# ScalarE's order in a recurrence over batches: two copies ahead of the next normalising

## The chip, the core and the metric

The kernel runs on one core of a Trainium2 chip. The metric is the device time of one execution in microseconds; the lower the better. The core has five instruction queues that run by themselves and meet only at semaphores: TensorE (PE, with its weight loads as PEld), VectorE (DVE), ScalarE (ACT), GpSimd (POOL) and SyncE (SP). Each queue is worked off strictly in the order in which it was written.

## The reference, cut to what matters

The input x has 8 batches of 512 rows of 128 values. Three layers follow one another: a mixture of experts, a linear recurrence along the rows, and the mixture of experts again with the same weights.

```python
x = x + 0.5 * ffn(layernorm(x), gate_w, w1, w2)
x = x + attn(layernorm(x), a_params, B_w, C_w, D)
x = x + 0.5 * ffn(layernorm(x), gate_w, w1, w2)

def attn(u, ...):            # per batch; W is a circulant matrix, so it is diagonal after an FFT
    Bu = einsum('bsd,nd->bsn', u, B_w)
    h_t = ifft(lambdas * fft(h_{t-1})).real + Bu_t
    return einsum('sbn,dn->bsd', hs, C_w) + D * u

def ffn(tokens, ...):        # 8 experts, each token to its best one, at most 160 tokens an expert
    logits = tokens @ gate_w; probs = softmax(logits); expert = argmax(probs)
    pos = running count of the tokens of that expert
    out = probs[expert] * relu(token @ w1[expert]) @ w2[expert]   # if pos < 160
```

## The kernel before

The first expert layer fills the first 62 us, the recurrence the stretch from 62 to about 120, and the second expert layer the rest. The change touches the recurrence alone.

The recurrence is worked in the frequency domain, where every state is one complex number that is turned by a fixed angle at each step. A batch is cut into 128 groups (NG) of 4 rows (TB). The state at the group boundaries comes from a scan over group sums that have been turned back to a common origin, and the rows within a group come from small tables. For each batch b of the 8 (NB) this happens, in this order of data:

- VectorE, `stats(b)`: mean and variance of the rows (sstat, smv). ScalarE, `deviation(b)`: the square root (ssd, L433). VectorE, `shift(b)`: reciprocal and shift (srs, snb, L715 and L716).
- ScalarE, `normalise(b)`: u, four instructions of 128x128 (L440). TensorE, `turn_u(b)`: four transposes into bank 4 (L977). ScalarE, `copy_uT(b)`: uT, one copy of 128x512 (L427).
- TensorE, `group_sums(b)`: the sums of the groups into bank 5 (L986, four matmuls that the trace counts as eight).
- ScalarE, `turned_part(b)`: two copies of 64x128 that swap the real and imaginary halves of bank 5 into vq (L419, L420). They need the group sums (semaphore v_ps) and GpSimd's product of the batch before (vb_r).
- VectorE, `turn_back(b)`: va = bank 5 times cosines (L722), once vq is there. GpSimd: vb = vq times sines (L339).
- VectorE, `carry(b)`: the scan z over va and vb (L730), then zs (L734). GpSimd: zc (L344). VectorE, `turn_forth(b)`: state = zc + zs (L743).
- TensorE, `read_out(b)`: state times a table into the batch's pair of banks (L1020), on top of `within_pairs(b)` (L997 to L1001) and `within_rest(b)` (L1008 to L1012), the products within the groups.
- VectorE, `add_back(b)` (L748) and `gate_back(b)` (L758, L761): the result with the residual, and the logits of the second expert layer. SP stores each batch.

The order of each queue is written out by hand. VectorE's loop for batch i is `turn_back(i)`, `stats(i + 2)`, `carry(i)`, `turn_forth(i)`, `add_back(i - 1)`, `gate_back(i - 1)`, `shift(i + 2)`, and in batches 3 to 6 a share of the routing of the second expert layer (`mark`, L540 to L587, and `make_hot`, L604 to L623). TensorE's loop is `group_sums(i)`, `read_out(i - 1)`, `within_pairs(i)`, `turn_u(i + 1)`, `within_rest(i)`; after batch 5 it ranks the first routed piece (`rank`, L864 to L871), after batch 7 it places it (`place`, L879), then ranks the second and reads out the last batch. `within_pairs(i)` waits until VectorE has read the batch two before it out of the same banks. GpSimd's loop is vb of the batch, then zc of the batch. `keep_warm` (L804) issues matmuls whose result is not used.

After the recurrence the last routing steps follow one another on VectorE and TensorE, then an indirect load by GpSimd (L317), then the experts (L910, L921).

Of the kernel before, what the change touches and what calls it, by code (L numbers as in the profile page):

```python
# [5 lines left out]
def macaron_moe_ssm_kernel(nc, x_in, x_turned, a_params, b_w, c_w, c_w_turned, d_skip, gate_w, w1, w2,  # L6
# [11 lines left out]

    NB, SEQ, D = x_in.shape
    E, _, F = w1.shape  # L20
    P = 128
    T = NB * SEQ
# [24 lines left out]
    with ctx:  # L47
# [301 lines left out]
        def _(act):  # L349
# [33 lines left out]
            def slots(n):  # L383
                def slot_in(j):
                    act.wait_ge(slotT_ps, n * NS + j + 1)
                    nc.scalar.copy(xcT[:, j * P:(j + 1) * P],  # L386
                                   bank[j % 2][:, 0:P]).then_inc(slotT_sb, 1)

                def relu(e):
                    for half in range(2):  # L390
                        act.wait_ge(h_ps, n * 2 * E + 2 * e + half + 1)
                        if e >= 2:
                            act.wait_ge(eo_ps, n * E + e - 1)
                        nc.scalar.activation(hT[:, e % 2, half * HC:(half + 1) * HC, :],  # L394
                                             bank[4 + half][:, 0:HC * CAP]
                                             .rearrange("p (c s) -> p c s", c=HC), ACT.Relu).then_inc(h_sb, 1)

                for kind, i in act_steps:
                    if kind == "i":
                        slot_in(i)  # L400
                    elif kind == "g":
                        act.wait_ge(rated, n * NS + NS)
                        nc.scalar.activation(gsd[:, :], gmv[:, :, 1], ACT.Sqrt, bias=eps[:, 0:1]).then_inc(gsd_r, 1)
                        nc.scalar.activation(table_load[:, 1:2], eps[:, 0:1], ACT.Exp)
                    elif kind == "e":
                        act.wait_ge(lg_r, n + 1)
                        nc.scalar.activation(pe_[:, :, :], lg[:, :, :], ACT.Exp).then_inc(pe_r, 1)
                    else:
                        relu(i)
# [3 lines left out]
            def turned_part(b):  # L413

                act.wait_ge(v_ps, b + 1)
                if b >= 1:
                    act.wait_ge(vb_r, b)
                v = bank[5][:, 0:NG]
                nc.scalar.copy(vq[0:P // 2, :], v[P // 2:P, :])  # L419
                nc.scalar.copy(vq[P // 2:P, :], v[0:P // 2, :]).then_inc(vq_sb, 1)  # L420

            def copy_uT(b):

                act.wait_ge(uT_ps, b + 1)
                if b >= 2:
                    act.wait_ge(lag_ps, b - 1)
                nc.scalar.copy(uT[:, b % 2, :], bank[4][:, :]).then_inc(uT_sb, 1)  # L427

            def deviation(b):
                act.wait_ge(svar, b + 1)  # L430
                if b >= 4:
                    act.wait_ge(y_read, b - 3)
                nc.scalar.activation(ssd[:, b % 4, :], smv[:, b % 2, :, 1], ACT.Sqrt, bias=eps[:, 0:1]).then_inc(ssd_r, 1)  # L433

            def normalise(b):
                act.wait_ge(snb_r, b + 1)
                if b >= 2:
                    act.wait_ge(uT_ps, b - 1)
                for c in range(TB):
                    ins = nc.scalar.activation(u[:, b % 2, c, :], x1[:, b * TB + c, :], ACT.Identity,  # L440
                                               bias=snb[:, b % 2, c:c + 1], scale=srs[:, b % 2, c:c + 1])
                ins.then_inc(u_r, 1)
# [3 lines left out]
            normalise(0)  # L446
            copy_uT(0)
            normalise(1)
            for i in range(NB):
                turned_part(i)  # L450
                if i + 1 < NB:
                    copy_uT(i + 1)
                if i + 2 < NB:
                    deviation(i + 2)
                    normalise(i + 2)
            slots(1)

# [648 lines left out]
```

## Time and profile before

| | us |
|---|---|
| median of 3 runs | 175.39 |
| lowest and highest | 174.82, 181.41 |
| the profiled execution | 176.61 |
| its span, first to last instruction | 174.7 |

The profile is of one execution. Times within it are microseconds from the first instruction. TensorE's clock has two levels, 1.2 and 2.4 GHz; a granted clock of 1.00 is the upper one and 0.50 the lower. Busy shares over the span are 80% for TensorE, 51% for VectorE, 33% for ScalarE and 30% for GpSimd.

### The profile page before, as it was taken

The page shows a single profiled execution, that of the slowest core. Times are in us where ns is not written, and L with a number is a line of the kernel's source. Part 1 is how long each engine was busy: PE and PEld are TensorE (multiplying, and loading weights), DVE is VectorE, ACT ScalarE, POOL GpSimd, SP SyncE. Part 2 cuts the span into 40 slices and gives each one's busy share as a digit, 9 for nine tenths or more (in the row PEclk, how much of TensorE's full clock was granted, in tenths as well). Part 3 has the DMA queues.
Part 4 walks back from the last instruction along what each step waited for, and adds up shares of the span by engine and source line. Part 5 has one row for each costly group of instructions (what it writes and reads, how often), then busy time and mean ns, then how long its engine had stood idle before and what let it go on. Part 6 is the DMA issues. An engine that isn't in the chain of part 4 may idle for free.

```text
span 174.7 us, 2535 instructions
## 1 busy us (share of the span) xinstructions
PE 140.6 (80%) x788; PEld 104.8 (60%) x791; DVE 89.7 (51%) x396; ACT 58.2 (33%) x144; POOL 52.9 (30%) x80
## 2 busy tenths in 40 slices
PE   6977899989999787499788888896439969999920
PEld 2137468389998432388566666675234448999810
DVE  1069762984474206065485597698464134434320
ACT  3421143634736000846525525510000013483200
POOL 3700001776047720022012012121000477305771
PEclk9998589999999999999999999999555987999995
DMA  4999990111001129300101100111010011100110
GB/s 133 314 364 362 372 560 19 45 45 51 9 19 58 51 51 323 141 2 0 60 25 39 60 38 23 62 60 64 0 60 0 13 47 45 45 4 31 46 45 30
DMA packets 11309, 16.21 MB, mean 93 GB/s; under 512 B 1665, under 2 KB 6273, under 8 KB 11265
## 3 DMA queue, kind: packets, MB, share of 16 engines
q1 hardware_dynamic: 9504, 13.11, 21.4%
q0 software_dynamic: 1280, 2.62, 5.0%
q10 hardware_dynamic: 512, 0.33, 0.7%
q8 instruction: 6, 0.10, 0.2%
q14 instruction: 7, 0.05, 0.1%
HBM read 12.65 MB, written 5.51 MB: 104 GB/s over the span
## 4 chain that ended last, share of the span: by engine, by line
PE 41%; DVE 24%; issue 10%; ACT 8%; DMA 8%; POOL 5%; SPq 1%; POOLq 1%; DVEq 0%; ACTq 0%
PE pair L910 11%; PE pair L921 9%; ACT u L440 5%; PE pair L852 5%; DVE sstat L701 4%; PE pair L879 4%; DMA xt<-x_turned 3%; PE pair L804 3%; DVE x L748 2%; PE pair L899 2%; POOL zc L344 2%; DVE smv L706 2%; DVE z L730 2%; DMA x<-x_scratch 2%; DMA xg<-out,tok 2%
## 5 line engine op out<-in xcount | busy, mean ns | idle before, releaser
L804 PE MATMUL pair<-warm_in,ones_bf 128*128 128x512 bf16 x77 | 21.7, 428 | 4.2 <-DVE warm_in L469 1.6
L910 PE MATMUL pair<-xcT,w1s 128*128 128x160 f32 x128 | 21.8, 316 | 0.0
L921 PE MATMUL pair<-hT,w2s 128*128 128x160 f32 x128 | 20.5, 303 | 0.8 <-ACT hT L394 0.8
L910 PEld LDWEIGHTS pair<-xcT,w1s 128*128 128x128 f32 x128 | 18.9, 199 | 0.8 <-ACT xcT L386 0.8
L394 ACT ACTIVATE hT<-pair 128x320 f32<-128x320 f32 x32 | 13.7, 436 | 16.4 <-PE pair L910 15.0
L921 PEld LDWEIGHTS pair<-hT,w2s 128*128 128x128 f32 x128 | 18.1, 192 | 1.5 <-ACT hT L394 0.8
L440 ACT ACTIVATE u<-x,snb,srs 128x128 f32<-128x128 f32 x32 | 13.2, 482 | 13.4 <-DVE snb L716 13.4
L317 POOL DMA_INDIRECT xg<-x,tok x10 | 10.2, 1024 | 23.7 <-DVE tok L638 20.9
L317 POOL DMA_INDIRECT xg<-out,tok x10 | 10.1, 1006 | 22.0 <-DVE tok L638 19.2
L804 PEld LDWEIGHTS pair<-warm_in,ones_bf 128*128 128x128 bf16 x80 | 8.3, 110 | 13.7 <-issue 3.3
L386 ACT COPY xcT<-pair 128x128 f32<-128x128 f32 x20 | 4.9, 266 | 31.3 <-PE pair L894 31.2
L339 POOL TENSOR_TENSOR vb<-vq,st 128x128 f32<-128x128 f32 x8 | 3.6, 455 | 37.3 <-ACT vq L420 37.3
L1020 PE MATMUL pair<-gt,state 128*128 128x272 f32 x32 | 10.4, 453 | 3.8 <-DVE state L743 3.8
L326 POOL DMA_INDIRECT out<-xnew,tok x10 | 9.9, 988 | 10.7 <-DVE xnew L682 8.9
L326 POOL DMA_INDIRECT x_scratch<-xnew,tok x10 | 9.9, 986 | 9.8 <-DVE xnew L682 7.9
L645 DVE BATCH_NORM_STATS2 gstat<-xg 128x6 f32<-128x128 f32 x20 | 5.7, 287 | 12.4 <-DMA xg<-out,tok 9.2
L879 PEld LDWEIGHTS pair<-hot_tok,hot_place 128*64 128x64 f16 x64 | 7.4, 202 | 7.8 <-DVE hot_place L623 6.1
L879 PE MATMUL pair<-hot_tok,hot_place 128*64 128x20 f16 x64 | 7.8, 265 | 5.3 <-DVE hot_place L623 5.3
L701 DVE BATCH_NORM_STATS2 sstat<-x 128x6 f32<-128x128 f32 x32 | 6.9, 278 | 6.9 <-DMA x<-x_scratch 6.9
L722 DVE TENSOR_TENSOR va<-pair,ct 128x128 f32<-128x128 f32 x8 | 2.3, 291 | 15.1 <-ACT vq L420 15.1
L672 DVE COPY eoT<-pair 128x160 f32<-128x160 f32 x16 | 5.1, 318 | 9.3 <-PE pair L921 9.3
L852 PE MATMUL pair<-w1s,center 128*128 128x512 f32 x16 | 9.6, 754 | 0.0
(170 smaller groups left out, 247.1 us busy)
## 6 DMA issues: line engine op xcount, KB each, us to landing
xt<-x_turned SPq DMA_DIRECT2D x8, 256.0 KB, 6.0
w1s<-w SPq DMA_DIRECT2D x2, 1024.0 KB, 7.5
w2s<-w SPq DMA_DIRECT2D x8, 256.0 KB, 6.7
x<-x_scratch SPq DMA_DIRECT2D x8, 256.0 KB, 4.5
out<-x SPq DMA_DIRECT2D x8, 256.0 KB, 2.0
ce<-const_early ACTq DMA_DIRECT2D x1, 318.0 KB, 4.4
cl<-const_late SPq DMA_DIRECT2D x1, 256.0 KB, 5.5
xg<-x,tok POOLq DMA_INDIRECT x10, 2.6
```

The lines of the kernel that those rows point to most:

```text
L317: pool.indirect_dma_start(xg[:, j, :], None, (x_rows, out_rows)[n], bass.IndirectOffsetOnAxis(ap=tok[:, j:j + 1], axis=0), bounds_check=T ...
L326: pool.indirect_dma_start((x1_dram, out_rows)[n], bass.IndirectOffsetOnAxis(ap=tok[:, j:j + 1], axis=0), xnew[:, j, :], None, bounds_check ...
L394: nc.scalar.activation(hT[:, e % 2, half * HC:(half + 1) * HC, :], bank[4 + half][:, 0:HC * CAP] .rearrange("p (c s) -> p c s", c=HC), ACT ...
L440: ins = nc.scalar.activation(u[:, b % 2, c, :], x1[:, b * TB + c, :], ACT.Identity, bias=snb[:, b % 2, c:c + 1], scale=srs[:, b % 2, c:c + 1])
L645: link(V.bn_stats(gstat[:, j, :], xg[:, j, :]))
L701: ins = V.bn_stats(sstat[:, b % 2, c, :], x1[:, b * TB + c, :])
L804: M(bank[to][:, :], ones_bf[:, :], warm_in[:, :], start=True, stop=True)
L852: M(bank[e % 2][:, :], center[:, :], w1s[:, e, :], start=True, stop=True).then_inc(w1c_ps, 1)
L879: ins = M(bank[7][0:SW, 0:NSTRIP], hot_place[:, :, t], hot_tok[:, :, t], start=(t == 0), stop=(t == NT - 1))
L910: ins = M(bank[4 + half][:, c * CAP:(c + 1) * CAP], w1s[:, i, ch * P:(ch + 1) * P], xcT[:, i * CAP:(i + 1) * CAP], start=True, stop=True)
L921: ins = M(bank[6 + i % 2][:, 0:CAP], w2s[:, i, c, :], hT[:, i % 2, c, :], start=(c == 0), stop=(c == FC - 1))
L1020: ins = M(y[:, h, E:E + 2 * PITCH], state[:, b % 2, :], gt[:, 2 * h:2 * h + 2, :].rearrange("p r c -> p (r c)"), start=False, stop=True, s ...
```

## The change

In ScalarE's loop over the batches, the two copies of batch i + 1 (`turned_part`) are issued ahead of `normalise(i + 2)`, where before they were issued after it, as the first step of the next round. The same instructions are issued, as often as before, on the same data and with the same semaphores. ScalarE's order before is copies 0, uT 1, deviation 2, normalise 2, copies 1, uT 2, deviation 3, normalise 3, copies 2 and so on; after the change it is copies 0, uT 1, deviation 2, copies 1, normalise 2, uT 2, deviation 3, copies 2, normalise 3 and so on.

```diff
             normalise(0)
             copy_uT(0)
             normalise(1)
+            turned_part(0)
             for i in range(NB):
-                turned_part(i)
                 if i + 1 < NB:
                     copy_uT(i + 1)
                 if i + 2 < NB:
                     deviation(i + 2)
+                if i + 1 < NB:
+                    turned_part(i + 1)
+                if i + 2 < NB:
                     normalise(i + 2)
             slots(1)
```

## Rows read from the trace of the kernel before

**Rows 1.** The page: TensorE's granted clock in 40 slices of 4.4 us, in tenths.

```profile
PEclk9998589999999999999999999999555987999995
```

**Rows 2.** Table of waits, 82 to 126 us: total, times, longest.

```profile
POOL vb L339 <- ACT vq L420: 21.5, 6, 4.1
ACT u L440 <- DVE snb L716: 12.0, 5, 2.4
```

**Rows 3.** Chain of waits, 92 to 107 us: shares by line, then start, us, what.

```profile
by line: ACT u L440 25.3%; DVE sstat L701 14.8%; issue 11.9%; DVE x L748 8.0%; POOL zc L344 7.6%; ACT vq L420 5.3%; ACT vq L419 5.2%; DVE smv L706 4.7%; DVE z L730 4.3%; DVE state L743 3.9%; DVE srs L715 2.5%; DVE lgu L758 2.3%; DVE snb L71
```

**Rows 4.** Timeline, ScalarE: start, us, engine, line, instruction, count [idle before, releaser].

```profile
78.38 1.65 ACT L440 ACTIVATE u<-x,snb,srs 128x128 f32<-128x128 f32 x4 [1.41 <-DVE snb L716]
...
99.69 0.26 ACT L420 COPY vq<-pair 64x128 f32<-64x128 f32 x1
...
104.26 1.65 ACT L440 ACTIVATE u<-x,snb,srs 128x128 f32<-128x128 f32 x4 [2.40 <-DVE snb L716]
105.93 0.26 ACT L419 COPY vq<-pair 64x128 f32<-64x128 f32 x1
106.20 0.26 ACT L420 COPY vq<-pair 64x128 f32<-64x128 f32 x1
```

**Rows 5.** Timeline, TensorE, from the group sums of batch 1 to those of 2.

```profile
76.86 1.05 PE L986 MATMUL pair<-uT,vt 128*128 128x128 f32 x8
...
78.11 1.18 PE L1020 MATMUL pair<-gt,state 128*128 128x272 f32 x4 [0.20 <-DVE state L743]
...
80.31 0.60 PE L977 MATMUL pair<-ce,u 128*128 128x128 f32 x4
...
81.92 1.05 PE L986 MATMUL pair<-uT,vt 128*128 128x128 f32 x8
```

**Rows 6.** Timeline, VectorE (and GpSimd's vb), batches 4 to 7.

```profile
100.05 0.29 DVE L722 TENSOR_TENSOR va<-pair,ct 128x128 f32<-128x128 f32 x1 [1.89 <-ACT vq L420]
...
104.06 0.16 DVE L716 SCALAR_TENSOR_TENSOR snb<-smv,srs 128x4 f32<-128x4 f32 x1
...
105.28 0.36 DVE L587 TENSOR_TENSOR_SCAN counted<-restart,chosen 128x96 bf16<-128x96 bf16 x1
...
106.50 0.29 DVE L722 TENSOR_TENSOR va<-pair,ct 128x128 f32<-128x128 f32 x1 [0.86 <-ACT vq L420]
...
111.80 0.17 DVE L614 TENSOR_SCALAR split_i<-slot_i 128x12 int16<-128x12 int16 x1
...
113.00 0.46 POOL L339 TENSOR_TENSOR vb<-vq,st 128x128 f32<-128x128 f32 x1 [4.07 <-ACT vq L420]
113.02 0.29 DVE L722 TENSOR_TENSOR va<-pair,ct 128x128 f32<-128x128 f32 x1 [1.05 <-ACT vq L420]
...
113.54 0.43 DVE L730 TENSOR_TENSOR_SCAN z<-va,vb 128x128 f32<-128x128 f32 x1 [0.23 <-POOL vb L339]
...
117.40 0.43 DVE L730 TENSOR_TENSOR_SCAN z<-va,vb 128x128 f32<-128x128 f32 x1
```

**Rows 7.** Timeline, TensorE, the ranking of piece 1 and the last read-out.

```profile
121.96 0.22 PE L864 MATMUL pair<-counted,ones_bf 128*128 128x96 bf16 x1 [1.73 <-DVE counted L587]
...
122.19 2.15 PE L1020 MATMUL pair<-gt,state 128*128 128x272 f32 x4
```

**Rows 8.** Stretches: length, busy (x count) of PE, PEld, DVE, ACT, POOL; PEclk, DMA, GB/s.

```profile
122.00:123.00 1.00, 1.00 (x6) 0.88 (x7) 0.00 (x0) 0.00 (x0) 0.00 (x0) 0.53 0.00 0
...
143.00:146.00 3.00, 2.69 (x11) 2.23 (x10) 1.29 (x6) 1.03 (x3) 2.38 (x3) 0.51 0.16 44
```

**Rows 9.** Timeline, the tail: the last placing and its operand; expert matmuls.

```profile
133.28 0.42 DVE L623 TENSOR_TENSOR hot_place<-split_i,place_no 128x512 f16<-128x512 int16 x1
...
134.85 1.06 PE L879 MATMUL pair<-hot_tok,hot_place 128*64 128x20 f16 x8
...
142.45 2.45 PE L910 MATMUL pair<-xcT,w1s 128*128 128x160 f32 x8
...
146.96 1.25 PE L910 MATMUL pair<-xcT,w1s 128*128 128x160 f32 x8
```

## The prediction

> **What bounds the kernel now.** I read four views, from the coarse to the fine. The page says that no engine is full over the span and that TensorE's clock is at its upper level all through the recurrence, slices 15 to 27 [rows 1]. Utilisation therefore decides nothing there; the order of waits does. The table of waits for the recurrence is next: GpSimd stands before its first product for ScalarE's copies, 21.5 us in six batches, while ScalarE stands for VectorE's snb before normalising, 12.0 us in five [rows 2]. Each waits for the other in turn: that is a ring. The chain of waits for two batches shows it closed: normalising is its largest link, a quarter of the stretch, and the two copies follow it directly [rows 3]. In the timeline, normalising of batch 6 runs from 104.26 to 105.91, the copies of batch 5 from 105.93 to 106.46, with nothing between them; the copies of batch 4 ended at 99.95, so one batch takes 6.51 us [rows 4]. Yet the group sums that those copies turn leave TensorE much earlier. In batch 1, they ended at 77.91 (76.86 + 1.05) [rows 5], before normalising of batch 2 was done. So the copies wait for nothing that they read: they wait for their place in ScalarE's queue.
>
> The ring now, from rows: VectorE from va to snb 4.17 (100.05 to 104.22) [rows 6], hand-over 0.04, four normalisings 1.65, hand-over 0.02, two copies 0.53, hand-over 0.10 (99.95 to 100.05). Sum 6.51, as measured. The account is complete. For hand-overs that the change makes new I take 0.05 between engines and 0.02 within one.
>
> **The change, part by part.** It moves two copies (0.53 us together) ahead of four normalisings (1.65 us). It adds and removes no instruction, no DMA and no semaphore; nothing moves on SP, GpSimd, VectorE or TensorE. Four edits follow from the one.
>
> (a) The copies leave the ring of VectorE and normalising. For batch 1 they now start when the group sums are there: 77.91 + 0.05 = 77.96, done 78.49, and va of batch 1 starts at 78.55.
>
> (b) A new wait stands ahead of normalising: ScalarE stands for the group sums of the batch before. Queued behind that wait are the four normalisings, the transposes on TensorE that read u, and the next copy of uT. For batch 2 this costs little: normalising would start at 78.38 as before [rows 4], the copies hold it to 78.51, so u ends at 80.16; TensorE is not free for those transposes before 80.31 anyway [rows 5]. The 0.13 is hidden by TensorE's own queue. So the group sums of batch 2 end as before, at 82.97, its copies at 83.55, and va starts at 83.60.
>
> (c) From there a new ring decides: transposes to the end of the group sums 2.66 (80.31 to 82.97) [rows 5], hand-over 0.05, copies 0.53, hand-over 0.02, normalising 1.65, hand-over 0.05. Sum 4.96. TensorE's own queue is nearly as long: group sums to group sums 5.06 with a 0.20 wait in it [rows 5], so 4.86. I take 4.96 for the ring; below 4.86 it can't go. VectorE's 4.17 is shorter for plain batches. Then va of batch 3 starts at 88.56 and of batch 4 at 93.52.
>
> (d) VectorE has routing work in later batches, and there its order becomes the bound. In batch 4, va to the end of counted is 5.59 (100.05 to 105.64) [rows 6]; with 0.03 between instructions, va of batch 5 starts at 99.14. In batch 5, va to the end of split_i is 5.47 (106.50 to 111.97): batch 6 at 104.64. Its group sums should end at 103.1 (82.97 + 4 x 4.96, and some 0.25 for the ranking matmuls ahead of them, as those of piece 1 delay the next matmul by 0.23, 121.96 to 122.19 [rows 7]), copies 103.7, hence VectorE is indeed later. Batch 6: va to z was 0.52, of which 0.23 was a wait for GpSimd's vb that goes away, so z starts at 104.93; from there to the next z VectorE works without a wait, 3.86 (113.54 to 117.40), which would be 108.79. The copies of batch 7: normalising can start at 103.7 and ends at 105.4, group sums 2.66 later at 108.1, copies 108.64. vb ends at 109.15 (0.05 and 0.46), and the scan z of batch 7 starts 0.08 later (113.46 to 113.54), at 109.2: here GpSimd is the later one. Before, it started at 117.40 [rows 6]. **The recurrence gives 8.2 us.**
>
> After that scan nothing is reordered, so the lead is carried through routing, gather and experts, with one term more, from TensorE's clock. Before, TensorE had nothing for 1.73 us ahead of the ranking of piece 1 [rows 7]; the second that follows had a mean clock of 0.53 [rows 8], and the four matmuls of the last read-out took 2.15 us, against 1.18 for the same four at the full clock [rows 5, 7]. They are on the path: VectorE waits for them. Now TensorE's queue runs later against VectorE's: after the group sums of batch 7 (108.1) come read-out and the products within the batch, 3.2 (the 4.86 of a batch less group sums 1.05 and transposes 0.60), and twelve placing matmuls, 1.6 (eight take 1.06 [rows 9]), to 112.9, while ranking follows z by the same 4.56 as before (117.40 to 121.96), at 113.8. The gap is 0.9 us in place of 1.73. I take the full rate for the read-out: 0.9 us gained. Its other bound is 0, if the clock falls at the same instruction.
>
> [...]
>
> Sum: 8.2 + 0.9 = 9.1 us. The profiled execution took 176.61 us, 1.9 more than its span; it would take 167.5. It lies 1.22 above the median of the runs, 175.39, and since the terms are differences, the forecast for the median is 175.39 - 9.1 = **166.3 us**.
>
> **The rivals.**
>
> *The tail meets a kinder clock.* Everything after the recurrence comes 8 us sooner, and the tail has two stretches at the lower level. In one, the last placing matmuls start at 134.85, although their operand was written by 133.70: they stood 1.15 behind keep-warm matmuls at half rate [rows 9]. In the other, 143 to 146 at 0.51 [rows 8], eight matmuls of expert 0 took 2.45 against 1.25 [rows 9], 1.20 more. Both spared: 163.9. For it: the smaller gap. Against it: the long wait after the last read-out remains, in which the clock had already fallen.
>
> *The tail meets a harder clock.* The read-out stays at half (0.9 back) and one more block of eight runs at half (1.2): 168.4. With two such blocks, 169.6. For it: only the order of work is fixed, not when the clock changes.
>
> *VectorE is the bound in every batch.* If its queue took 5.6 us in all batches instead of in the routed ones, va of batch 7 would come at 78.55 + 6 x 5.6 = 112.15 and z at 112.5, so the recurrence gives 4.9 and the time is 170.5 without the clock's term. Against it: 4.17 in a plain batch is a row without waits in it.
>
> *The gain is given back.* The expert stage would need 5.6 us more, five blocks at half instead of one or two: about 172.3 (166.3 + 5 x 1.2), no measurable change. A change that does nothing belongs here too (175.4): for that the group sums would have to be late, and 77.91 is against it.
>
> *Slower.* The new wait ties normalising to TensorE's pace, so a halved clock inside the recurrence would now count in full. The read-out's ratio, 2.15 / 1.18 = 1.82, makes TensorE's 4.86 into 8.85 us a batch, 3.9 over the new ring. From the fourth such batch on, the gain and the 2% are gone (9.1 + 3.5 = 12.6 against 4 x 3.9 = 15.6): 181.9. Against it: the clock is full there now, with more idle time of TensorE than afterwards.
>
> **How the numbers follow.** About 2% (3.5 us) is what a measurement of this kernel can tell from no change. Forecast, 165 to 168: 0.62. Kinder clock, 163 to 165: 0.14. Harder clock, 168 to 170: 0.13. VectorE in every batch: 0.03. Given back, or nothing done: 0.05. Slower: 0.03. All but the last two lie over 2% below 175.39, so faster 0.92, same 0.05, slower 0.03. The range runs from both clock gains (163.9, less half a microsecond for the runs' scatter) to two blocks at half (169.6, rounded up): 163.4 to 169.8. What it leaves out holds under 2 in 10.
>
> **What the profile after would show.** (a) ScalarE's two copies start some 0.05 after TensorE's group sums, with that as releaser, and no longer right after normalising. (b) Normalising starts right after the copies; the wait for snb nearly vanishes from the table and a wait for the group sums takes its place. (c) Batches 2 to 4 are about 5.0 us apart. (d) In batches 4 to 6 VectorE has no wait ahead of va, and the spacing of va is 5.6 and 5.5. The last scan starts near 109. The last read-out takes 1.2, not 2.15. The prediction is wrong if the spacing in (c) stays above 6, if group sums start late because of something in TensorE's queue that the slack of before covered, or if the granted clock in the expert stage differs for more than two blocks.

## The result, and the profile after

The changed kernel took 168.28 us (median of 4 runs, 167.04 to 169.97), against 176.44 for the kernel before beside it (median of 4, 174.82 to 181.41). The ratio is 0.9587, with a 95% interval of 0.9479 to 0.9695. In a second comparison on another occasion, the same kernel gave 0.9464 (0.9382 to 0.9545). The forecast was 166.3 us, a ratio of 0.948 to the 175.39 that it started from. Executions in which TensorE's clock is lower over the whole span are longer by some per cent for every kernel here; the ratios leave them out.

The profiled execution after took 168.07 us, with a span of 166.0, against 176.61 and 174.7 before.

First the page of the changed kernel: its span and the granted clock, to be laid beside [rows 1].

```profile
span 166.0 us, 2535 instructions
...
PEclk9998579999999999987999999999755699999995
```

A dip that was not there before stands in slices 17 and 18, at the start of the recurrence; the one in the expert stage of before (its slices 34 and 35) is missing.

The table of waits of the changed kernel, 78 to 110 us: who waited for whom, total, times, longest.

```profile
POOL vb L339 <- ACT vq L420: 15.3, 6, 2.7
ACT vq L419 <- PE pair L989: 9.4, 7, 1.5
```

The row of [rows 2] in which ScalarE waited for VectorE's snb is gone. In its place ScalarE now waits for the group sums, 1.3 us a batch. GpSimd's longest wait for the copies has gone from 4.1 to 2.7 us.

The chain of waits, 85 to 96 us (line numbers below the change are three higher): shares, then start, us, what.

```profile
by line: ACT u L440 30.1%; PE pair L989 16.5%; PE pair L980 11.9%; issue 11.3%; PE pair L1013 8.6%; PE pair L1011 8.4%; DVE sstat L704 7.9%; PE pair L1015 4.5%; ACT vq L420 2.7%; DVE va L725 1.6%; ACT vq L419 0.4%; DVEq L724 0.2%
...
85.00 1.66 ACT u L440 x4
...
86.70 0.66 PE pair L980 x4
87.36 0.46 PE pair L1011 x2
87.82 0.47 PE pair L1013 x2
88.29 0.24 PE pair L1015 x2
88.54 0.91 PE pair L989 x8
...
90.02 1.66 ACT u L440 x4
```

Beside [rows 3]: the round between two normalisings no longer passes through VectorE's scan, state and snb; it passes through the transposes, the rest of the products within the batch (L1011 to L1015) and the group sums, all on TensorE. One round goes from normalising at 85.00 to normalising at 90.02, 5.02 us.

Timeline of ScalarE, batches 1 and 2, answering to [rows 4], and of TensorE, answering to [rows 5].

```profile
78.33 1.05 PE L989 MATMUL pair<-uT,vt 128*128 128x128 f32 x8
...
83.36 1.05 PE L989 MATMUL pair<-uT,vt 128*128 128x128 f32 x8
...
84.25 1.08 PE L1023 MATMUL pair<-gt,state 128*128 128x272 f32 x4
...
84.45 0.26 ACT L419 COPY vq<-pair 64x128 f32<-64x128 f32 x1 [1.29 <-PE pair L989]
84.72 0.26 ACT L420 COPY vq<-pair 64x128 f32<-64x128 f32 x1
85.00 1.65 ACT L440 ACTIVATE u<-x,snb,srs 128x128 f32<-128x128 f32 x4
...
86.70 0.66 PE L980 MATMUL pair<-ce,u 128*128 128x128 f32 x4 [0.20 <-ACT u L440]
```

The copies start 0.04 after the group sums (83.36 + 1.05 = 84.41) and normalising follows them at once.

VectorE's va of batches 4 to 7 and the last scan, answering to [rows 6].

```profile
95.11 0.29 DVE L725 TENSOR_TENSOR va<-pair,ct 128x128 f32<-128x128 f32 x1 [0.45 <-ACT vq L420]
...
100.70 0.26 DVE L725 TENSOR_TENSOR va<-pair,ct 128x128 f32<-128x128 f32 x1
...
106.38 0.29 DVE L725 TENSOR_TENSOR va<-pair,ct 128x128 f32<-128x128 f32 x1
...
110.28 0.29 DVE L725 TENSOR_TENSOR va<-pair,ct 128x128 f32<-128x128 f32 x1
...
110.86 0.42 DVE L733 TENSOR_TENSOR_SCAN z<-va,vb 128x128 f32<-128x128 f32 x1 [0.30 <-POOL vb L339]
```

The tail on TensorE, answering to [rows 7] and [rows 9]: ranking and last read-out, the placing after them, the last placing, and the first two blocks of expert matmuls.

```profile
115.43 0.22 PE L867 MATMUL pair<-counted,ones_bf 128*128 128x96 bf16 x1 [1.05 <-DVE counted L590]
...
115.60 1.15 PE L1023 MATMUL pair<-gt,state 128*128 128x272 f32 x4
122.06 1.50 PE L882 MATMUL pair<-hot_tok,hot_place 128*64 128x20 f16 x12 [5.32 <-DVE hot_place L626]
...
127.26 1.06 PE L882 MATMUL pair<-hot_tok,hot_place 128*64 128x20 f16 x8
...
134.79 1.35 PE L913 MATMUL pair<-xcT,w1s 128*128 128x160 f32 x8
...
137.97 1.25 PE L913 MATMUL pair<-xcT,w1s 128*128 128x160 f32 x8
```

And the stretch with the dip in the changed kernel, with the rest of the recurrence (columns as in [rows 8]).

```profile
73.00:77.00 4.00, 4.00 (x18) 3.50 (x19) 1.98 (x11) 1.88 (x6) 0.63 (x2) 0.59 0.00 0
...
78.00:116.00 38.00, 35.76 (x217) 30.65 (x216) 31.53 (x137) 18.14 (x50) 7.10 (x14) 1.00 0.13 49
```

The table goes through the two profiles from one landmark to the next. Its last column is what the changed kernel gained between the landmark above and this one, in us.

| landmark | before | after | gained here |
|---|---|---|---|
| group sums of batch 2 start | 81.92 | 83.36 | -1.44 |
| last scan z | 117.40 | 110.86 | +7.98 |
| placing of piece 1 | 129.66 | 122.06 | +1.06 |
| first block of expert matmuls | 142.45 | 134.79 | +0.06 |
| second such block | 146.96 | 137.97 | +1.33 |
| end | 174.7 | 166.0 | -0.29 |

The sum is 8.70. The order of ScalarE gave 7.98 of it. The three terms -1.44, +1.06 and +1.33 come from TensorE's clock, which was lower in one place and higher in two: group sums 0 to 1 took 5.46 in place of 3.78 at the start (1.68, of which 0.21 was made good by transposes that began earlier), the last read-out 1.15 in place of 2.15, and the first block of expert matmuls 1.35 in place of 2.45.

### The profile page after: what moved, and what is told of

The parts are those of the page before. It is cut to its first block, busy times and chain, and to the rows that moved or that the text cites. A ratio compares the mean times of both kernels' runs of the same rounds, so it can differ in the third digit from the quotient of the medians.

```text
span 166.0 us, 2535 instructions
## 1 busy us (share of the span) xinstructions
PE 139.0 (84%) x788; PEld 105.1 (63%) x791; DVE 89.9 (54%) x396; ACT 57.5 (35%) x144; POOL 52.9 (32%) x80
## 3 DMA queue, kind: packets, MB, share of 16 engines
q0 software_dynamic: 1280, 2.62, 5.3%
## 4 chain that ended last, share of the span: by engine, by line
PE 45%; DVE 18%; issue 11%; DMA 8%; POOL 8%; ACT 5%; SPq 1%; POOLq 1%; DVEq 0%
PE pair L913 8%; PE pair L924 8%; PE pair L855 5%; ACT u L440 4%; PE pair L882 4%; DMA xt<-x_turned 4%; POOL xg L317 4%; PE pair L989 3%; PE pair L807 3%; PE pair L980 2%; DVE sstat L704 2%; DVE chosen L554 2%; DMA x<-x_scratch 2%; PE pair L902 2%; DMA xg<-out,tok 1%
## 5 line engine op out<-in xcount | busy, mean ns | idle before, releaser
L807 PE MATMUL pair<-warm_in,ones_bf 128*128 128x512 bf16 x77 | 23.3, 455 | 4.4 <-DMA x<-x_scratch 1.7
L913 PE MATMUL pair<-xcT,w1s 128*128 128x160 f32 x128 | 20.7, 305 | 0.0
L913 PEld LDWEIGHTS pair<-xcT,w1s 128*128 128x128 f32 x128 | 18.0, 190 | 0.8 <-ACT xcT L386 0.8
L989 PE MATMUL pair<-uT,vt 128*128 128x128 f32 x64 | 8.8, 281 | 0.7 <-ACT uT L427 0.7
L685 DVE SCALAR_TENSOR_TENSOR xnew<-pair,gscale,xg 128x128 f32<-128x128 f32 x20 | 6.4, 347 | 5.3 <-PE pair L933 5.2
```

The source lines that it names most:

```text
L685: V.scalar_tensor_tensor(xnew[:, i, :], bank[2 + i % 2][:, 0:P], gscale[:, i:i + 1], xg[:, i, :], ALU.mult, ALU.add).then_inc(row_sb, 1)
L807: M(bank[to][:, :], ones_bf[:, :], warm_in[:, :], start=True, stop=True)
L913: ins = M(bank[4 + half][:, c * CAP:(c + 1) * CAP], w1s[:, i, ch * P:(ch + 1) * P], xcT[:, i * CAP:(i + 1) * CAP], start=True, stop=True)
L989: ins = M(bank[5][:, 0:NG], vt[:, TB - 1 - c, :], uT[:, b % 2, c * P:(c + 1) * P], start=(c == 0), stop=(c == TB - 1))
```

## The experiments

The yardstick is the stretch from the start of the group sums of batch 2 to the last scan z. The granted clock was 1.00 over it in every profile, so no difference in it is one of the clock. It was 35.48 us in the kernel before, 27.50 in the changed kernel and 27.52 when the changed kernel was profiled again. (For kernels in the old order, whose first batches differ, it goes from va of batch 1: 36.78 before.)

| kernel | batch to batch | stretch | against the changed kernel |
|---|---|---|---|
| new order for three batches | 5.02, then 6.5 | 30.56 | +3.06 |
| copy added in the ring | 5.54 | 30.12 | +2.62 |
| copy added ahead of the wait | 5.02 | 27.51 | 0.0 |
| deviation behind the copies | 5.81 | 31.49 | +3.99 |
| VectorE loaded in plain batches | 5.02 | 27.52 | 0.0 |
| VectorE loaded in routed batches | 5.02 | 28.51 | +1.01 |
| finer handover | 4.69 | 26.36 | -1.14 |

**The new order for three batches only.**

```diff
-                if i + 1 < NB:
+                if i + 1 < NB and i < 3:
                     turned_part(i + 1)
                 if i + 2 < NB:
                     normalise(i + 2)
+                if i + 1 < NB and i >= 3:
+                    turned_part(i + 1)
```

> The changed kernel, with the new order for the copies of batches 1 to 3 only; those of batches 4 to 7 stand behind the normalising again. Ring theory (each batch in the new order goes at 5.0 us, each in the old one at 6.5): the spacing of va is 5.0 up to batch 3 and 6.5 again from batch 4 to 6; from va of batch 4 to the last scan 17.3 us as before, not 15.7. The last scan comes 3.1 us later than in the changed kernel, so some 171 us. Rival, one lead that is gained once (the copies of batch 1 being early) and then kept: the last scan within 1 us of the changed kernel's. Rival, TensorE's clock made the difference and not the order: no clear step in the spacing at batch 4.

The stretch grew by 3.06, and va went 5.02 apart up to batch 3, then 6.52, 6.46 and 6.52. ScalarE's timeline in this kernel shows the switch from one ring to the other:

```profile
88.56 0.26 ACT L420 COPY vq<-pair 64x128 f32<-64x128 f32 x1
88.85 1.65 ACT L440 ACTIVATE u<-x,snb,srs 128x128 f32<-128x128 f32 x4
...
93.08 1.65 ACT L440 ACTIVATE u<-x,snb,srs 128x128 f32<-128x128 f32 x4 [1.05 <-DVE snb L721]
94.75 0.26 ACT L419 COPY vq<-pair 64x128 f32<-64x128 f32 x1
```

Above, normalising follows the copies; below, it waits for snb again and the copies follow it. The clock was full on both sides of the switch, which rules out the clock as the cause; that the gain stops where the order stops rules out a lead won once. The profiled execution took 169.88 us, against the 171 expected; the four runs scatter from 169.4 to 178.8, so no ratio is used.

**One more copy, in two places.** In both, a copy of uT, 128x512, into a scratch tile, in six batches:

```diff
                 if i + 2 < NB:
                     deviation(i + 2)
+                    nc.scalar.copy(pad_out[:, :], uT[:, i % 2, :])   # one kernel: ahead of the wait
                 if i + 1 < NB:
                     turned_part(i + 1)
                 if i + 2 < NB:
+                    nc.scalar.copy(pad_out[:, :], uT[:, i % 2, :])   # the other: in the ring
                     normalise(i + 2)
```

> The changed kernel with one more ScalarE instruction a batch, a copy of 128x512 into a scratch tile that nobody reads, between the two copies and the four normalisings (six in all). Ring theory: this place is on the new ring, which has no slack; group sums to group sums goes from 5.02 by the whole length of the copy (about 0.6) to 5.6, and the last scan is 2.5 to 3.0 us later than in the changed kernel. Rival, VectorE is the bound now (its queue takes 5.6 in the batches with routing): those batches absorb it, 1.2 us or less in all. Rival, TensorE's queue (4.9 a batch) is the bound: it absorbs 0.1 of each copy, and this can hardly be told from the ring.

> The same additional copy, as often, but ahead of the two copies, right behind the deviation, where ScalarE stands 1.29 us for the group sums. Ring theory: nothing is later, group sums stay 5.02 apart, the time is that of the changed kernel within its scatter. Rival, ScalarE's total work decides (its queue is as loaded as with the copy in the other place): the same 2.5 to 3.0 us as there.

In the ring the batches went 5.54 apart, 0.52 more; the copy lasts 0.62 and overlaps its successor by 0.10. Ahead of the wait they stayed at 5.02. First the copy in the ring, then the one ahead of the wait:

```profile
87.63 0.62 ACT L459 COPY pad_out<-uT 128x512 f32<-128x512 f32 x1
88.15 1.64 ACT L441 ACTIVATE u<-x,snb,srs 128x128 f32<-128x128 f32 x4
```

```profile
80.71 0.61 ACT L456 COPY pad_out<-uT 128x512 f32<-128x512 f32 x1
82.10 0.26 ACT L420 COPY vq<-pair 64x128 f32<-64x128 f32 x1 [0.78 <-PE pair L991]
```

The same instruction cost 2.62 us in the one place and nothing in the other, where it only shortened the wait from 1.29 to 0.78. Order, not load, is ScalarE's limit. The VectorE rival said 1.2 or less and falls. So does the rival that TensorE's queue absorbs 0.1 of each copy: TensorE's wait for u ahead of the transposes grew from 0.20 to 0.72, by the same 0.52 by which normalising came later. In times: 175.93 us (174.4 to 177.8) and 169.11 (166.9 to 176.5; ratio 0.9622, 0.9466 to 0.9777), against 176.22 for the kernel before. The time of the kernel with the copy in the ring holds more than the copy: its profiled span, 172.4, is 6.4 longer than the 166.0 of the changed kernel, of which 2.62 lie in the stretch and 0.51 between group sums 1 and 2. Most of the rest is a later arrival at the first transposes (0.86) and the clock: 1.09 more from group sums 0 to 1, and a last read-out of 2.15.

**The copies one place further ahead.**

```diff
                 if i + 1 < NB:
                     copy_uT(i + 1)
+                    turned_part(i + 1)
                 if i + 2 < NB:
                     deviation(i + 2)
-                if i + 1 < NB:
-                    turned_part(i + 1)
-                if i + 2 < NB:
                     normalise(i + 2)
```

> The changed kernel with the copies one place further ahead: ahead of the deviation of batch b + 2 as well, directly behind the copy of uT. Ring theory: the copies start no sooner, since they wait for the group sums, but the deviation (0.30) now comes behind them, and VectorE's reciprocal and shift (0.18 and 0.16 with hand-overs, 0.5 in all) behind that, and only then normalising: the ring becomes 5.02 + 0.32 + 0.45 = 5.8 us, and the last scan is 3 to 4 us later than in the changed kernel (VectorE's routing of 5.6 no longer shows). Rival, the deviation is covered wherever it stands: 5.02 as it was. Rival, what the change won came from the copies being as early as possible: a little faster still.

5.81 apart, as worked out, and half of what the order had gained in the stretch is gone (3.99 of 7.98): ratio 0.9826 (0.9694 to 0.9959). ScalarE's timeline:

```profile
89.44 0.26 ACT L420 COPY vq<-pair 64x128 f32<-64x128 f32 x1
89.72 0.30 ACT L433 ACTIVATE ssd<-smv,eps 128x4 f32<-128x4 f32 x1
90.52 1.65 ACT L440 ACTIVATE u<-x,snb,srs 128x128 f32<-128x128 f32 x4 [0.50 <-DVE snb L717]
```

What was free ahead of the wait costs its own 0.30 and VectorE's 0.50 behind it.

**VectorE with more to do.** A sum of 128x512 into a scratch tile at the end of batches 1 and 2 in one kernel, 4 and 5 in the other:

```diff
+                if i in (1, 2):        # the other kernel: (4, 5)
+                    V.tensor_tensor(pad_out[...], x1[:, 0:TB, :], x1[:, TB:2 * TB, :], ALU.add)
                 if i == ROUTE_FROM:
                     mark(1, 0, (True, False))
```

> The changed kernel with one more VectorE instruction (a sum of 128x512 into a scratch tile, about 0.6 us) at the end of batches 1 and 2, where VectorE waits 0.84 us for the copies. Ring theory: it fits into the wait, va stays 5.02 apart, from group sums 2 to the last scan 27.5 us. Rival, VectorE is the bound in plain batches: 1.2 us later.

> The same instruction at the end of batches 4 and 5, which carry routing work and where VectorE had no wait ahead of va. If VectorE sets the pace there, as forecast, va goes 5.6 + 0.6 and 5.7 + 0.6 apart and the last scan comes 1.2 us later: 28.7 us from group sums 2. Rival, the ring through ScalarE and TensorE runs beside it with as much behind it, so that only part arrives: under 0.6.

In plain batches it cost nothing (27.52). In the routed ones, va went 6.19 and 6.34 apart in place of 5.59 and 5.68, and the last scan came 1.01 later, where 1.2 was expected; of the 1.26 at va, about 0.3 went into the scan's wait for vb, which is no longer there. So VectorE sets the pace in the routed batches, and only there. (The times, 171.8 and 171.9 us in the median, scatter by 5 to 8 us and decide nothing at this size.) The timeline of the second kernel:

```profile
94.72 0.29 DVE L726 TENSOR_TENSOR va<-pair,ct 128x128 f32<-128x128 f32 x1 [0.45 <-ACT vq L421]
...
100.91 0.26 DVE L726 TENSOR_TENSOR va<-pair,ct 128x128 f32<-128x128 f32 x1
...
107.25 0.29 DVE L726 TENSOR_TENSOR va<-pair,ct 128x128 f32<-128x128 f32 x1
```

**A finer handover, in either order.** One semaphore count for each normalising:

```diff
                 for c in range(TB):
                     ins = nc.scalar.activation(u[:, b % 2, c, :], ...)
-                ins.then_inc(u_r, 1)
+                    ins.then_inc(u_r, 1)
...
-                pe.wait_ge(u_r, b + 1)
                 if b >= 1:
                     pe.wait_ge(uT_sb, b)
                 for c in range(TB):
+                    pe.wait_ge(u_r, TB * b + c + 1)
```

(and VectorE's wait in `shift` counts TB times as far).

> The changed kernel with one semaphore count for each of the four normalisings instead of one for all; each of the four transposes of a batch waits for its own. Ring theory: the first three transposes go below the normalising, so the ring loses some 0.4 us, falls below TensorE's own queue, and TensorE becomes the bound: group sums to group sums 4.86 to 4.9 instead of 5.02, TensorE with no wait for u in it, the last scan 0.5 to 0.9 us earlier. Rival, VectorE is the bound: no difference at the last scan. Rival, four waits cost more than they free: the spacing grows by the four waits, 0.1 to 0.2.

> The kernel before, with only the finer handover (one count for each normalising, the transposes waiting one by one). Ring theory: in the old order the transposes are not on the ring (normalising, copies, VectorE up to snb), so TensorE's transposes and group sums come 0.4 us sooner and nothing follows from it: va stays 6.45 to 6.5 apart, the time that of before. Rival, the finer handover gains by itself whatever the order: batches 0.3 us shorter, 2 us in all.

On the changed kernel, batches went 4.69 apart, and in the stretch from 82 to 96 us TensorE has no wait for u left: its queue is the bound. The floor of 4.86 that I had put there was too high. The stretch is 1.14 shorter, more than the 0.5 to 0.9 expected; 0.20 of it is batch 5, which took 5.48 in place of 5.68 for a reason of its own (last section). The time does not show the gain: the ratio is 0.9525 (0.9441 to 0.9609), and the changed kernel had 0.9464 (0.9382 to 0.9545) on the same occasion. The 1.14 rests on the trace alone. On the kernel before, va stayed 6.45 apart (va 1 to the last scan 36.64, against 36.78), ratio 1.0011 (0.9942 to 1.0080), although the transposes now overlap normalising there too:

```profile
99.75 1.65 ACT L440 ACTIVATE u<-x,snb,srs 128x128 f32<-128x128 f32 x4 [2.40 <-DVE snb L716]
...
100.82 0.95 PE L977 MATMUL pair<-ce,u 128*128 128x128 f32 x4
101.42 0.26 ACT L419 COPY vq<-pair 64x128 f32<-64x128 f32 x1
...
102.05 0.29 DVE L722 TENSOR_TENSOR va<-pair,ct 128x128 f32<-128x128 f32 x1 [1.88 <-ACT vq L420]
```

The transposes begin 0.6 before normalising ends, and nobody on the ring waits for them. In the traces it is an improvement that exists only after the change.

**The clock.** Three kernels: the changed one as it is, once more; with keep-warm matmuls at the start of the recurrence; and the kernel before with six of them in the gap ahead of the last read-out.

```diff
-            keep_warm(14, 6)
+            keep_warm(22, 6)              # changed kernel
...
+            keep_warm(6)                  # kernel before
             rank(1, 1)
             read_out(NB - 1)
```

> The changed kernel, unaltered. Order theory: group sums 5.02 apart whatever the clock does elsewhere, and the sum of recurrence and clocks gives a time of 0.96 of before. What it tells apart: if the half-rate stretch at the start of the recurrence (73 to 77 us in the first profile) belongs to the change, it is here again; if it is a matter of the execution, it is elsewhere or absent, and the time to the group sums of batch 1 is 1.5 us shorter.

> The changed kernel with 22 instead of 14 keep-warm matmuls between the arrival of the first rows and the first transposes. In the first profile TensorE was idle there for 2.00 us and its clock was at half from 73 to 77, which cost 1.5 us up to the group sums of batch 1; in the profile of before it was idle as long and the clock stayed at full. Clock theory: without the gap the clock doesn't fall there, and such executions gain 1.5 us; those in which it did not fall anyway gain nothing, so 0 to 1.5 in the median. Rival, the half rate there has another cause: it shows in spite of the matmuls. Loss possible: none up to 70.7 us, when they end.

> The kernel before, with six keep-warm matmuls ahead of the ranking of piece 1, in the 1.73 us in which TensorE had nothing to do. Clock theory (the clock fell in that gap, and the fall made the last read-out 2.15 instead of 1.2 us): the read-out takes 1.2 and the time falls by 0.9 us against before. Rival, the clock falls there for what came earlier: the read-out stays at 2.15 and nothing is gained. The order of ScalarE is untouched, so batches stay 6.5 us apart.

The half rate at the start was there again in the second profile of the changed kernel (granted clock 0.57 from 74 to 78 us), and the order in the ring was the same to 0.02 us. It is no property of the new order, though. Without more keep-warm matmuls there are twelve profiles: of the nine with the copies moved (all or some of them), five had it and four did not; of the three in the old order, one had it. Where the clock fell, group sums 0 to 1 took 5.46 to 6.55 us in place of 3.79.

The gap itself is another matter. TensorE's idle time ahead of the first transposes was 2.0 us in ten of the twelve, and six of these ten had the half rate. In the two with the finer handover it was 0.84, since the first transpose waits for one normalising only, and neither had the half rate. With 22 matmuls it was 0.27 in one kernel and nothing in the next, and the clock stayed up in both. So none of four fell behind a shorter gap, against six of ten behind the long one. That speaks for the gap, but if it played no part, chance would put all six falls among those ten in about 1 case of 14 (210 of 3003 ways). The ratio with 22 matmuls is 0.9504 (0.9421 to 0.9588), no better than the 0.9464 of the changed kernel beside it.

In the kernel before with the gap filled, the read-out took 1.15, as the clock theory wanted, and the placing came 1.05 sooner after the last scan (11.21 in place of 12.26); the time can't tell: 0.9985 (0.9911 to 1.0059) holds both no change and the 0.9 us (0.5%) expected. But the other runs take the explanation away. These are ranking and read-out, first in the kernel with the copy in the ring, then in the one with VectorE loaded in the routed batches:

```profile
120.66 0.26 PE L869 MATMUL pair<-counted,ones_bf 128*128 128x96 bf16 x1 [1.05 <-DVE counted L592]
...
120.93 2.15 PE L1025 MATMUL pair<-gt,state 128*128 128x272 f32 x4
```

```profile
116.02 0.22 PE L871 MATMUL pair<-counted,ones_bf 128*128 128x96 bf16 x1 [1.75 <-DVE counted L591]
...
116.19 1.15 PE L1027 MATMUL pair<-gt,state 128*128 128x272 f32 x4
```

A gap of 1.05 with the half rate behind it, one of 1.75 with the full rate. The length of this gap does not decide alone. Of the thirteen profiles in which it was not filled (1.05 to 1.75 us), the read-out took 1.15 to 1.17 in nine, 2.15 in two, and 1.38 and 1.57 in the two kernels with 22 matmuls at the start, where the clock fell while it ran. No run tells whether those matmuls had a part in that.

**Both additions.** The changed kernel with the finer handover and the 22 matmuls.

> The changed kernel with both additions: one count for each normalising, and 22 keep-warm matmuls at the start. The first run of the first gave group sums 4.69 apart, not 4.86, and a last scan 1.1 us earlier against the group sums of batch 2; the second had no half rate at the start. If they add up: 4.69 again, the clock at full from the first transposes on, from group sums 2 to the last scan 26.4 us, and a time of about 0.945 of before. If the clock at the start is chance and not the gap, it may fall here too.

In the recurrence they add up: 4.69 apart, 26.34 from group sums 2 to the last scan, full clock at the start. It took 166.53 us (165.09 to 169.64) against 176.84, ratio 0.9410 (0.9345 to 0.9474). This is the lowest ratio here, and the trace puts the stretch 1.16 us ahead of the changed kernel; but the interval overlaps with that of the changed kernel in the second comparison (0.9382 to 0.9545), so the times do not tell the two apart.

## Why the prediction was right, point by point

The time lay in the range and its cause was the one forecast; 166.3 was 2.0 below the median measured. About half of the 2.0 is the starting point: the kernel before had 176.44 beside the changed one, and the forecast had started from 175.39. The other half is the size: 9.1 forecast, 8.16 between the two medians. At 168.28 the time even lies just above the likeliest band, in the one that was given to a harder clock in the tail; that is not what happened, since the tail's clock was kinder.

- **The old ring** of 6.51 and the claim that the copies wait only for their place: shown by the kernel with the new order in three batches, where each batch goes by its own order.
- **(a)** The copies start 0.04 after the group sums; 0.05 was taken.
- **(b)** The cost for batch 2 was hidden where the clock was full: group sums 1 to 2 took 5.06 to 5.07 in such profiles, 5.06 before.
- **(c)** The new ring was 5.02, forecast 4.96. The 0.06 lie between the start of the transposes and the end of the group sums, 2.72 (86.70 to 89.42) in place of the 2.66 of [rows 5]: there the transposes had not waited and took 0.60, here they follow a wait and take 0.66. The floor under the ring was mis-sized: 4.86 came from taking the 0.20 of [rows 5] as all the idle time of TensorE. That figure counts from the modelled end of the group sums; started back to back, the read-out comes 0.89 after their start (83.36 to 84.25 in the changed kernel), so the wait was 0.36. TensorE's queue showed its true length, 4.69, only when the finer handover made it the bound.
- **(d)** From va of batch 4 to the next, 5.62 was forecast and 5.59 measured; from batch 5, 5.50 and 5.68 (last section). The sign given for (d), no wait ahead of va in batches 4 to 6, held for 5 and 6. Batch 4 had one of 0.45, as it should by the working in (c), where va of batch 4 still goes by the ring. At the last scan GpSimd's vb was the later one, as forecast, with a wait of 0.30.
- **The sum of the recurrence** was 8.2, measured 7.98 from the group sums of batch 2 on. From va of batch 2 to va of batch 4 it took 10.10, forecast 9.92; from there to va of batch 6 11.27, forecast 11.12; the rest was 0.11 shorter than forecast.
- **The clock's term** of 0.9 was of the right size (2.15 to 1.15), but its reason did not hold: the gap did shrink, to 1.05, and yet one of 1.05 was seen with the half rate behind it and one of 1.75 with the full rate. That the read-out ran at full rate in this profile was luck. The rule of "TensorE: Matmul & The Clock Gate" in the Trainium skill ("Why this matters for your kernels") asks for no idle gaps between bursts of matmuls above a stated length, and both 1.73 and 1.05 lie below it. So it does not say which of the two costs the clock, and the trace before, where the clock fell behind 1.73, is no case of it.
- **What was missing** is the start. I took the recurrence's clock as given because [rows 1] showed it full; in the profile after, 1.44 was lost there. It is the same sort of term as the two of the tail, and it should have stood among the rivals. The kinder clock in the expert stage (1.33) made up for it, which was luck too: the three terms of the clock, -1.44, +1.06 and +1.33, sum to 0.95, next to the 0.9 forecast, though only one of the three was forecast.
- **The rivals.** The kinder clock came in part: the block of expert matmuls was spared, the 1.15 ahead of the last placing was not (operand written by 126.11, placing at 127.26). VectorE in every batch falls (no cost of 0.68 us more in plain batches). Slower needed four batches at half; none of the recurrence from batch 2 on was at half in any profile.

## What to carry to other kernels

In a loop over several in-order queues, write down the ring: who hands to whom, with durations, until the sum equals the measured period. Then look for a step on the ring that waits for its place and not for its data, and put it where its queue already waits. What stands ahead of such a wait is free up to its length, and what is put behind it counts in full: the same copy cost 0 and 2.6 us. After such a change, look again: the finer handover that brought nothing before made the recurrence 1.1 us shorter in the trace afterwards. A gain of that size has to be read from a stretch of the trace, since the times here do not resolve it.

## What the runs showed of the hardware

Two things I had not expected. First, VectorE's instructions grew longer beside GpSimd's product. The comparison of the counts against the capacity (`over`, 128x12) took 0.17 in the kernel before and 0.38 in the changed one, where vb ran at the same time; in the timeline, before and then after:

```profile
111.24 0.17 DVE L608 TENSOR_SCALAR over<-count 128x12 f32<-128x12 f32 x1
```

```profile
105.31 0.45 POOL L339 TENSOR_TENSOR vb<-vq,st 128x128 f32<-128x128 f32 x1 [2.21 <-ACT vq L420]
...
105.41 0.38 DVE L611 TENSOR_SCALAR over<-count 128x12 f32<-128x12 f32 x1
```

It ended at 105.79, vb at 105.76. Batch 5 was 0.18 longer than forecast: 0.21 more here, less 0.03 at va, which took 0.26 without a wait ahead of it.

No run changed this alone, but the kept profiles separate the two cases. In all five profiles in which this instruction began while vb ran, it ended 0.03 after vb, whether it had begun early and took 0.38 (four of them) or late and took 0.21 (VectorE loaded in plain batches). In the nine others it took 0.17. With the finer handover, vb was over by then, and batch 5 took 5.48:

```profile
102.27 0.48 POOL L339 TENSOR_TENSOR vb<-vq,st 128x128 f32<-128x128 f32 x1 [1.60 <-ACT vq L420]
...
102.98 0.17 DVE L611 TENSOR_SCALAR over<-count 128x12 f32<-128x12 f32 x1
```

The added sum of 128x512 took 0.82 where vb ran beside it and 0.68 alone. "SBUF — State Buffer" in the Trainium skill, under "Who interferes with whom", says that a VectorE instruction in a mode with two ports contends with GpSimd for a pair of ports that they share, and that one with two inputs in SBUF contends with a GpSimd instruction that reads SBUF, as vb does. The added sum has two such inputs and agrees with it. For the comparison, which has one, the lengthening agrees with the first of the two conditions; that it ran in such a mode was not shown.

Second, the clock fell in some profiles and stayed up in others behind the same gap, in kernels whose instructions were alike up to there: at the start of the recurrence, behind 2.0 us (six of ten, 1.7 to 2.8 us more from group sums 0 to 1), and at the last read-out, behind 1.05 (1.0 us); among the first experts it differed as well (2.45, 2.39 or 1.35 us for the first block). A difference of two profiled spans below some 3 us says nothing about a change until it is broken down by stretches at equal clock.
